# Values of the third attention formed in one go after the routing instead of tile by tile in the attention

## The reference

```python
x = x + jnp.tanh(g_ffn[1]) * _L1_ffn_ref(_layernorm(x, axis=-1), ...)      # 8 experts, 2 per token, by router scores
x = x + jnp.tanh(g_xattn[2]) * _L2_xattn_ref(_layernorm(x, axis=-1), ctx_1024, ctx_1024, ...)

def _L2_xattn_ref(q, k, v, W_q, b_q, W_k, b_k, W_v, b_v, W_o, b_o):
    qh = _split_heads(q @ W_q + b_q, B)
    kh = _split_heads(k @ W_k + b_k, B)
    vh = _split_heads(v @ W_v + b_v, B)
    scores = jnp.einsum('bhsd,bhtd->bhst', qh, kh) / jnp.sqrt(jnp.float32(D_K))
    attn = jax.nn.softmax(scores, axis=-1)
    out = jnp.einsum('bhst,bhtd->bhsd', attn, vh)
    return out.transpose(0, 2, 1, 3).reshape(B, -1, H * D_K) @ W_o + b_o
```

## Time and profile before

| | us |
|---|---|
| runs | 1035.28, 1035.51, 1038.65; median 1035.51 |
| profiled execution, own time | 1037.14 |
| its span in the profile | 1035.3 |
| PE busy | 909.9 (88%) |
| DVE busy | 841.2 (81%) |
| ACT busy | 677.7 (65%) |
| POOL busy | 578.2 (56%) |

### The profile page before, as it was taken

One profiled execution on the slowest core, in us unless ns is written; L12 is line 12 of the kernel. 1 busy time (PEld: TensorE's weight loads), 2 busy tenths in 40 slices (PEclk: granted clock), 3 DMA queues, 4 the chain that ended last, 5 costly groups with the idle time before them and its releaser, 6 DMA issues. The chain is left out here.

```text
span 1035.3 us, 30109 instructions
## 1 busy us (share of the span) xinstructions
PE 909.9 (88%) x11572; PEld 696.4 (67%) x11593; DVE 841.2 (81%) x2240; ACT 677.7 (65%) x1740; POOL 578.2 (56%) x736
## 2 busy tenths in 40 slices
PE   8999999999999980599958999997888999968775
PEld 5888879988888860276637888874446777733332
DVE  5999987878899984366648999987997999978987
ACT  5888874357777740154536777786876788856663
POOL 6444402343347767423158888714665478768884
PEclk9999999999999985799989999998999999969998
DMA  8670000000000001356311111000000000000000
GB/s 223 159 288 2 3 2 2 2 2 2 3 10 28 31 32 51 100 174 188 115 47 32 31 30 30 25 3 1 2 2 1 3 2 3 3 1 16 21 22 26
DMA packets 60527, 44.44 MB, mean 43 GB/s; under 512 B 15196, under 2 KB 55781, under 8 KB 59366
## 3 DMA queue, kind: packets, MB, share of 16 engines
q1 hardware_dynamic: 55718, 34.09, 11.1%
q0 software_dynamic: 4096, 8.34, 2.7%
q10 hardware_dynamic: 576, 0.13, 0.1%
HBM read 23.73 MB, written 18.87 MB: 41 GB/s over the span
## 5 line engine op out<-in xcount | busy, mean ns | idle before, releaser
L2111 DVE TENSOR_REDUCE rowmax<-ps 128x16 f32<-128x1024 f32 x128 | 155.4, 1214 | 27.2 <-PE ps L729 26.5
L1136 ACT ACTIVATE pr<-ps 128x512 f32<-128x512 f32 x256 | 139.0, 595 | 48.9 <-PE ps L798 45.5
L2117 DVE TENSOR_TENSOR sm<-ps,rowmax 128x512 f32<-128x512 f32 x256 | 164.9, 686 | 3.4
L798 PE MATMUL ps<-cst,sm 128*128 128x128 f32 x1024 | 142.0, 278 | 13.3 <-DVE sm L2117 9.6
L756 PE MATMUL ps<-vbd,pr 128*64 128x18 f32 x4096 | 141.7, 212 | 0.6 <-ACT pr L1136 0.5
L756 PEld LDWEIGHTS ps<-vbd,pr 128*64 128x64 f32 x4096 | 134.0, 138 | 5.2 <-ACT pr L1136 1.6
L798 PEld LDWEIGHTS ps<-cst,sm 128*128 128x128 f32 x1024 | 111.5, 141 | 32.5 <-issue 21.9
L1526 POOL TENSOR_SCALAR xn<-x_sb,mv_all,rstd_all 128x128 f32<-128x128 f32 x122 | 99.3, 814 | 35.8 <-PE ps L693 28.5
L1016 ACT ACTIVATE qbd<-ps,bqp,cst 128x128 f32<-128x128 f32 x256 | 104.8, 464 | 6.5 <-PE ps L709 2.7
L1313 POOL DMA_INDIRECT big<-expert_out,row_g x64 | 68.4, 1069 | 45.4 <-DMA expert_out<-xn_all 23.0
L1330 POOL DMA_INDIRECT slots<-xn_all,row_s x64 | 65.1, 1017 | 30.6 <-DVE sm L2117 15.9
(11 more groups left out here) (322 smaller groups left out, 2334.0 us busy)
## 6 DMA issues: line engine op xcount, KB each, us to landing
slots<-hT SPq DMA_DIRECT2D x8, 1024.0 KB, 10.7
sm<-slots SPq DMA_DIRECT2D x32, 256.0 KB, 3.2
expert_out<-xn_all SPq DMA_DIRECT2D x16, 256.0 KB, 2.9
ew<-in_L_ffn_w SPq DMA_DIRECT2D x24, 128.0 KB, 2.5
out<-x_sb SPq DMA_DIRECT2D x32, 64.0 KB, 1.5
slots<-xn_all,row_s POOLq DMA_INDIRECT x64
big<-expert_out,row_g POOLq DMA_INDIRECT x64
x_sb<-in_x SPq DMA_DIRECT2D x1, 512.0 KB, 4.5
```

Source lines behind the costliest of these rows:

```text
L798: last = nc.tensor.transpose(turned[b][:, r * P:(r + 1) * P], sm[x][:, c:c + P], ident)
L1136: nc.scalar.activation(pr[y][:, b, :], turned[b], ACT.Exp, scale=SCALE).then_inc(p_ready[y], 1)
L2111: v.tensor_reduce(row3, sc, AX.X, ALU.max).then_inc(rowmax_ready[x], 1)
L2117: v.tensor_tensor(sm[x][:, :].rearrange("p (r g k) -> p r g k", r=RG, k=S)[:, part], sc[:, part], row3[:, part].unsqueeze(3).broadcast_to( ...
```

## The change

`project_values(g)` is new: for each of eight groups of four tiles it forms the same products for attention 2 on TensorE, into bank 2 or 6 in turn, after the last routing step and before the wait for the scatters; ScalarE copies each group, 128x512, into the halves of `values2`, which are `amask` and columns 1024 to 3071 of `big`. In attention 2 the products are left out, with TensorE's wait for `v_taken` before the transposes, and `values` reads SBUF, behind a wait for `o_psum` of the tile two before, instead of for `v_psum`. `keep_clock` reads a stretch of the constants in place of `amask`.

```diff
+        values2 = [amask[:, :].bitcast(F32), big[:, 1024:1024 + T * P // 2]]
+
+        def values_of(t):
+            return values2[t // (T // 2)][:, t % (T // 2) * P:(t % (T // 2) + 1) * P]
...
-                    nc.tensor.matmul(out, ones_b[:, :], amask[:, 0:512], start=True, stop=True, skip_group_check=True)
+                    nc.tensor.matmul(out, ones_b[:, :], cst[:, C_ONE:C_ONE + 256].bitcast(BF16), start=True, stop=True, skip_group_check=True)
...
+            def project_values(g):
+                out = bank(g % 2, 2)
+                if g > 1:
+                    pe.wait_ge(v_psum[1], 2 * IT + g - 1)
+                for t in range(GROUP):
+                    last = value_products(2, g * GROUP + t, out[:, t * P:(t + 1) * P])
+                last.then_inc(v_psum[0], 1)
...
-                    if new is not None and l != 3:
+                    if new is not None and l < 2:
                         value_products(l, t, turned[1][:, 0:P]).then_inc(v_psum[x], 1)
...
-                        if l != 3:
+                        if l < 2:
                             pe.wait_ge(v_taken[x], IT * l + new + 1)
...
+            for g in range(GROUPS):
+                project_values(g)
+            pe.wait_ge(v_psum[1], 2 * IT + GROUPS)
...
-                    if new is not None and l == 3:
+                    if new is not None and l >= 2:
                         act.wait_ge(o_psum[x], IT * l + new)
-                        values(x, xn_all[:, t * P:(t + 1) * P])
+                        values(x, xn_all[:, t * P:(t + 1) * P] if l == 3 else values_of(t))
...
             load_table(ACT.Gelu_apprx_tanh)
+            for g in range(GROUPS):
+                act.wait_ge(v_psum[0], 2 * IT + g + 1)
+                nc.scalar.activation(group(values2[g // (GROUPS // 2)], g % (GROUPS // 2)), bank(g % 2, 2), ACT.Copy).then_inc(v_psum[1], 1)
```

## The result

The changed kernel took 1044.6 us (median of 5 runs, 1042.57 to 1047.3), the one before 1036.64 (5 runs, 1035.28 to 1038.65): ratio 1.0079, 95% interval 1.0066 to 1.0092. That is 8 us slower, where 1034.8 with a range of 1030.8 to 1036.8 was forecast. The profiled executions took 1045.27 and 1037.14, with spans of 1043.5 and 1035.3.

What follows compares the result with a forecast made beforehand. In the third attention's middle TensorE was taken to wait for VectorE, with GpSimd's list the second bound. The tail's 0.7 us off the 1035.3 span gave 1034.6, or 1034.8 from the runs' median; all other terms 0; range 1030.8 to 1036.8.

Steps and rivals of the forecast that it cites:

- added in the drain: cost 0: Drain: eight groups of products at 1.77 us and their copies end at 408.2, covered by 9 to 16 us, cost 0.
- The other end named for this step: Drain: if the cover were gone, 14.2 us of products would be on the path.
- D: Drain: products not done by 424, experts start late by 3 us or more, 1038 and up; chance 0.03.
- Its sign: Sign of D in the drain: the 18 clock matmuls come later than 424.
- L742 starts 0.64 after `sm` ends: Third attention's middle: the scores (L729 before the change) still start 0.64 us after `sm`, TensorE waiting for VectorE.
- starts with the end of the power: Third attention's middle: VectorE's reciprocal still starts at the end of GpSimd's power, in halves as long as before.
- A: Third attention: L772 holds VectorE's reciprocal, so 13 stops gain 0.23 each; 3.7 us with the tail, 1031.8; chance 0.12.
- B: Third attention: TensorE is the chain throughout, gaining 32 x 0.23 = 7.4 us, 1028.1; chance 0.06.
- The tail: Third attention, tiles 28 to 31: 2 x 0.23 plus 0.20 plus 0, a gain of 0.66 us.
- The middle: Third attention, tiles 1 to 26: gain 0, the scores already at their least distance from `sm`.
- the start: Third attention from tile 0: TensorE's gain is swallowed by GpSimd's gathers, 0; the other end a gain of 0.5 us.
- C: Third attention's start: granted clock rises later, two halves at half speed cost 5.4 us, 1040.2; chance 0.07.

Runs made afterwards that it cites:

- kind A: Chips, or their condition, on which the kernel before takes 1037 us, as in the recorded pair; the changed kernel's ratio there was 1.0074.
- kind B: Chips, or their condition, on which the kernel before takes 1029 us; the changed kernel's ratio there was 0.9984.
- e2: Changed kernel still forming the values in the drain, but the third attention forms and reads its own: 1028.04 us, ratio 0.9995 to before, kind B.
- e7: Changed kernel run again, unaltered, on kind B: 1026.92 us against 1029.05 for the kernel before, ratio 0.9984.
- e5: Changed kernel run again, unaltered, on kind A: 1044.89 us against 1036.98 for the kernel before, ratio 1.0074.
- e6: Kernel before run again for its trace, on e5's chip, kind A: third attention 142.73 us from the maximum of tile 0 to that of tile 31.
- e16: Changed kernel with the forming moved to the pause before the third attention and the eight clock matmuls behind it left out: 1036.25 us, ratio 0.9999, kind A.
- e17: Changed kernel plus six 512-column matmuls after the first group, rows dropped in the last 14 scatters, a second forming before the third attention: 1047.46 us, kind A.
- e15: Same kernel as e17, with its three probes added to the changed kernel, on kind B: 1030.63 us.
- e13: Same kernel as e17, with its three probes added to the changed kernel, on kind B: 1026.21 us.
- e1: Changed kernel without the forming in the drain, values copied from the transposed context and so wrong: 1026.27 us, ratio 0.9971 to before, kind B.

## Why the prediction was wrong

**The step that failed is "added in the drain: cost 0".** It took the duration of a group from 704 us, where GpSimd issues no indirect transfers, and TensorE's being free from 392.8 as its being able to work at that pace. What the runs put in its place on kind A: 42 of 256 loads at full pace, 16 in the next 30 us, 198 in 8.1 us after 427.26, then a copy and the 18 clock matmuls, 10.04 us late in all. The other end named for this step, 14.2, was the right order of size; it was kept out of the range on the strength of 9 to 16 us of cover, and cover counted in time is worth little where the engine starts 16 loads in 30 us. On kind B the step held: products and copies were over by 402.35 in e2 and 403.99 in e7, and the cost was nothing.

**The rival that came true is D** (products not done by 424, chance 0.03). Its sign was the one named, the clock matmuls at 436.22 and not at 424.27. Its place was named, its mechanism was not. Rows 7's "35 instructions in 9.29 us" was the hint: a loop without waits that is 30% busy.

**Right on kind A:** L742 starts 0.64 after `sm` ends in all 26 halves from tile 2 to 27 of the changed kernel. The reciprocal, where it is held, starts with the end of the power, L785 having ended 0.73 to 1.29 earlier; so A, that L772 holds it, falls for kind A. The Trainium skill ("SBUF — State Buffer", Who interferes with whom) says that a VectorE instruction with at most one SBUF input and outside the 2-port modes doesn't contend with GpSimd, which would have excluded GpSimd as holder through that port. On kind A the rows show the stop all the same, and what holds it is not shown; on kind B there is no stop to describe. B (7.4 us throughout) falls too: tiles 5 to 28 gained 1.25 on kind A, not 23 x 0.23 = 5.3. ScalarE's copies from SBUF take 309 ns, 310 were put down.

**The terms of the sum.** The tail: 12.76 to 12.10, 0.66, to the hundredth. (Tile 27, which the sum passes over, went from 0.70 to 0.64 as well; it counts in the middle.) The middle: 0 was forecast, 1.25 came on kind A (means of two traces and of four) and 0.7 on B. On B the rows give the reason. In e2 TensorE was late by 0.1 in most halves (L742 0.70 to 0.74 after `sm`), and the reciprocal came as its L785 ended. Timelines of e2, then of e7:
```profile
584.70 0.39 PE L785 MATMUL ps<-y_bias_b,cst 128*128 128x128 f32 x2
585.12 0.26 DVE L2064 RECIPROCAL rden<-ps 128x16 f32<-128x16 f32 x1
```
```profile
585.67 0.39 PE L785 MATMUL ps<-y_bias_b,cst 128*128 128x128 f32 x2
586.30 0.25 DVE L2064 RECIPROCAL rden<-ps 128x16 f32<-128x16 f32 x1
```

In e2 it starts 0.03 after L785, in e7 0.24 after, and from the reciprocal before (580.83, and 582.08) the halves take 4.29 and 4.22 us. So where GpSimd stops nothing, TensorE's list was the chain by 0.07 of the removed 0.23: rivals A and B hold there in small. What gives 1.25 on kind A is not settled; the stops fall otherwise, and before's own two traces differ by 0.9. Together with the start, the gain on kind B is 1.4 to 2.0 by the traces and 2.1 by the runs of e7, where 0.7 was forecast.

**C, the clock at the stage's start,** came in part. The granted clock of the changed kernel in 555 to 561 is 0.50, and in e5 it stays there to 571:
```profile
555.00:561.00 6.00, 5.09 (x31) 3.55 (x29) 4.00 (x9) 2.81 (x9) 5.26 (x7) 0.50 0.15 42
```
```profile
569.00:571.00 2.00, 2.00 (x15) 1.96 (x13) 0.48 (x3) 0.22 (x1) 1.19 (x2) 0.50 0.14 37
```

The first row is the recorded trace, the second e5 (columns as for the earlier trace rows). In before and e6 it is at 0.53 to 0.62 from 544 to 548 and at 1.00 after. Tiles 0 to 5 take 25.11 and 27.45 us against 24.69 and 24.42: 0.4 and 3.0 lost, and e5's profiled run, at 1047.71, is 2.8 above its median. In e16 and e17, whose products stand just before the stage, the clock is 1.00 from tile 0's maximum on and tiles 0 to 5 take 23.2. But e15 is the same kernel as e17, and there the clock stays at 0.50 from 546 to 561 and 5.1 us are lost against e13. So products ahead of the stage are no safeguard, the low clock belongs to neither kind, and what decides it is open. C was given 0.07 and 5.4 us; in the recorded pair it cost 0.4, at its worst 5.1.

The forecast thus had the drain and the sign right for a kind of chip that the recorded pair didn't run on (2.1 us faster there, 0.7 forecast), which is luck, since it was worked out from a trace of the other kind; for that one it was wrong.

## What to carry to other kernels

An engine that stands idle is not therefore free: before work is moved into a stretch, look in that stretch for any instruction of any engine that waits for nothing, and compare its pace with the same instruction elsewhere. Where GpSimd issues indirect transfers back to back, put little beside them, or time it on more than one chip; the same forming beside a short run of six gathers made the next stage 3.6 us late, where beside the drain's scatters it was 10. And time a close change on several chips before it is kept: this one is worth minus 2 or plus 8 us.

## What the runs showed of the hardware

- Two kinds of chip, or conditions of a chip. The same program takes 1029 or 1037 us. The 8 us stand in the third attention (134.6 in e2 against 142.7 to 143.9), where GpSimd gathers. The scatters' pace is the same on both (one per 1.28 us, 0.97 each), and the mean granted clock doesn't tell them apart (0.955 in the profiled runs of e1 and of e16). Why some chips have it is open.
- On kind A, while GpSimd issues indirect transfers back to back, TensorE and VectorE come to start an instruction only at some points of a grid of 0.70 us, and ScalarE started none for 30 us, though what its next one needs was done. Each engine first gets some at full pace: TensorE 42 loads when GpSimd had long been at it, 72 or 73 when GpSimd had just begun, VectorE eight additions. In the drain it ends 3.85 us after GpSimd's last transfer (423.41 to 427.26; in e17 422.17 to 426.03), on the engines that it holds within 0.11 us of each other (427.26, 427.28, 427.37).
- As far as the rows tell, it isn't for want of transferred instructions. In the changed kernel's drain the instruction queue moved one block between 393 and 397.3, and between 397.5 and 432 none but a small one on another queue. That one moves in 426 to 427, when the crawl ends, but in e7 too, where nothing crawled. The view of transfers of that stretch, the changed kernel first and then e7, which needed a block more since it didn't crawl:
```profile
q0 software_dynamic: 675, 1.33, 11.8%
...
q14 instruction: 1, 0.01, 0.1%
```
```profile
q0 software_dynamic: 672, 1.32, 11.8%
...
q8 instruction: 1, 0.02, 0.3%
q14 instruction: 1, 0.01, 0.1%
```

  So what ran on TensorE at full pace from 427.26 to 432 had been on the core while it crawled. The Trainium skill ("Runtime: NRT & Kernel Launch", Instruction fetch mechanics) says that such refills are mostly hidden; that agrees, and leaves the crawl unexplained. What GpSimd's handling of transfers shares with the engines' start of an instruction no run shows; that it is the writing of the profile's own records isn't excluded either.
